# Vision tower on one Trainium2 core: gate products moved into the second half of the image ahead, weighing runs behind the scores

## The chip, the cores and the metric

The kernel runs on one core of one Trainium2 chip. The metric is the device time of one execution, in microseconds (us). Engines are called PE (matmul), PEld (its weight loads), DVE, ACT, POOL and SP (which only issues DMAs).

## What is computed

Eight images of 3 x 512 x 512 go through a patch embedding, one attention layer with a gate, and a layer of eight experts of which one is chosen per token. Everything is fp32 (some matmul operands fp32r). The part that the change touches, cut from the reference:

```python
h = embed(x) + pos                                   # 1024 tokens an image, 256 wide
normed = layernorm(h) ; a = layernorm(normed)        # attention's own layer norm follows the first
q, k, v = split(a * gamma + beta) @ W_qkv.T          # 8 heads of 32
gate = sigmoid(normed @ W_gate.T + b_gate)
attn = softmax(q @ k.T * 32 ** -0.5)
out = einsum('bhij,bhid->bhjd', attn, v) * gate      # weighed over the query tokens i
h = h + normed + out @ W_final.T + b_final
h = h + expert(layernorm(h))                         # router: argmax of softmax(gelu(..) @ Wg)
```

## The kernel before, in words

The eight images are software-pipelined in `image(b, par, before, after)`, which each engine's program has. Image b is in attention; image b + 1 is embedded, normalised, turned and projected meanwhile (`after`); image b - 1 is finished: final product, layer norm, router and hidden layer (`before`). At the end come a sort of the tokens by expert and the expert products, which the change does not touch.

Attention runs in 64 steps (STEPS), one for a head and a tile of 128 tokens: k // 32 is the half (G_STEPS = 32; four heads each), (k % 32) // 4 the tile, k % 4 the head. In a step PE makes the score of 128 x 1024 (L509) in one of two pairs of banks (SR = 2), DVE its maximum (L1066, nmax), ACT the exponential into pr (L854) with its sum. The score of step k waits for the exponential of step k - 2, whose banks it takes. After four steps DVE divides v by the four sums (scale_v, L954 and L957, vs), and PE weighs with it (weigh, L523): 16 products j = 0 to 3 times four heads, in two runs of eight. What else runs in a step is set by tables:

- WEIGH_AT: the runs of group i come at the end of steps 4i + 5 and 4i + 7, behind the step's other work;
- QK1_AT: projections of q and k for the second half in steps 0 to 7; EMBED_AT: embedding of the next image in steps 8 to 31, three pieces a tile (L476, added to hres by DVE, L930);
- GATE_AT: in steps 35 to 38 the gate products of the second feature chunk (L543), each of two steps followed by a tanh on ACT (L803); those of the first chunk stand between the final products (L559) and step 0;
- TURN_AT: in steps 39 to 46 eight turns (L488, four transposes each) of the next image's n and a, read by ACT into nt (L783) and at (L786);
- QK0_AT: in steps 49 to 59 the next image's q and k for its first half (L497): eight products, in two of every three steps, high part by ACT (L797), low part by DVE (L945) two steps later; VALUE_AT: its values (L536) in steps 61 and 63.

Banks 6 and 7 (spare) serve all of that by turns: gates, turns, projections, embedding, values, final products. Each user waits for the reader of the one before.

Ahead of step 0, PE makes values, the last weighings of the image before, and its final products; DVE adds those to hres in four pieces (L973), then does statistics (L908, L915), and only then its first maximum. Ahead of step 32 stand norm_turn (L572, which waits until DVE has added the last embedding, emb_h), the weighing of group 7, and the router of the image before, some 30 us of PE work. SP loads the stacks st, which scores read, by `load_stack`: twelve DMAs, three a head, after the last low part and after the last score of the half before.

## Time and profile before

| | us |
|---|---|
| median of 3 runs | 1819.79 (1818.34 to 1821.87) |
| the profiled execution, its own time | 1824.39 |
| its span, first to last instruction | 1822.6 |
| busy in the span: PE, DVE, ACT, POOL | 1631.2, 1201.0, 943.0, 307.8 |
| mean granted TensorE clock | 0.967 |

A page gives each engine's busy time and the chain of work that ended last. Matmuls are pipelined and their ends modelled, so their rows overlap: the distance of two starts tells more than a row's length. A row of the timeline has start, length, engine, line, operation, output <- input, shapes, count, and in brackets the idle time before it with the engine and line that ended it. A stretch is a window (from:to), its length, the busy time and the number of records of PE, PEld, DVE, ACT and POOL, then the granted clock (PEclk), the DMA share and GB/s. The step of a row is found by counting exponentials.

### The profile page before, as it was taken

What the parts mean: (1) busy time and instruction counts of PE and PEld (TensorE: products, weight loads), DVE (VectorE), ACT (ScalarE), POOL (GpSimd) and SP (SyncE); (2) the same over time, 40 slices, a digit from 0 to 9 for tenths busy, and PEclk for the clock granted to TensorE, in tenths of its full rate; (3) what the DMA queues carried; (4) which work ended last, traced back from release to release, by engine and by line L of the source; (5) the groups of instructions that cost most, each with busy time, mean ns of one, the idle gap of its engine ahead of it and who ended that gap; (6) DMA issues with size and microseconds to landing.
All of it is one profiled execution on the core that took longest, in us unless ns stands there. A gap on an engine that the chain in (4) does not pass through costs nothing.

```text
span 1822.6 us, 29454 instructions
## 1 busy us (share of the span) xinstructions
PE 1631.2 (90%) x11124; PEld 1125.0 (62%) x11124; DVE 1201.0 (66%) x1904; ACT 943.0 (52%) x1560; POOL 307.8 (17%) x231
## 2 busy tenths in 40 slices
PE   8796999999999999999999999998885707999998
PEld 6463556556646665665657456645443506999998
DVE  2376686868777776777677767776666496444443
ACT  0465655756575657567565756575663331222222
POOL 0202000200200020002001000200000081555554
PEclk9798999999999999999999999999999858999999
DMA  4313235242604251342325141603330462666663
GB/s 162 87 53 69 43 94 132 57 99 64 144 19 111 68 147 23 106 117 81 87 67 131 42 110 53 162 5 89 80 83 20 118 163 90 199 202 204 208 198 129
DMA packets 121218, 187.57 MB, mean 103 GB/s; under 512 B 11883, under 2 KB 86265, under 8 KB 120956
## 3 DMA queue, kind: packets, MB, share of 16 engines
q1 hardware_dynamic: 104652, 120.42, 26.7%
q0 software_dynamic: 16000, 63.98, 10.9%
q8 instruction: 93, 1.52, 0.3%
q10 hardware_dynamic: 432, 1.31, 0.2%
q14 instruction: 41, 0.34, 0.1%
HBM read 84.98 MB, written 51.38 MB: 75 GB/s over the span
## 4 chain that ended last, share of the span: by engine, by line
PE 68%; DVE 18%; issue 7%; ACT 5%; DMA 1%; SPq 1%; POOL 0%; POOLq 0%; DVEq 0%; ACTq 0%
PE ps L509 12%; PE ps L752 11%; PE ps L523 11%; PE ps L476 8%; DVE nmax L1066 6%; ACT pr L854 3%; PE ps L740 3%; PE ps L559 3%; PE ps L536 3%; PE ps L497 3%; PE ps L580 2%; PE ps L582 2%; PE ps L581 2%; PE ps L543 1%; PE ps L450 1%
## 5 line engine op out<-in xcount | busy, mean ns | idle before, releaser
L1066 DVE TENSOR_REDUCE nmax<-ps 128x1 f32<-128x1024 f32 x512 | 623.7, 1221 | 216.7 <-PE ps L509 209.8
L854 ACT ACTIVATE pr<-ps,nmax 128x1024 f32<-128x1024 f32 x512 | 570.7, 1115 | 287.1 <-DVE nmax L1066 282.2
L509 PE MATMUL ps<-st 96*128 96x512 f32 x1024 | 399.6, 474 | 70.5 <-ACT pr L854 60.8
L509 PEld LDWEIGHTS ps<-st 96*128 96x128 f32 x1024 | 168.2, 191 | 266.5 <-ACT pr L854 128.6
L523 PE MATMUL ps<-pr,vs 128*32 128x256 f32 x4096 | 271.7, 386 | 11.5 <-DVE vs L957 11.5
L752 PE MATMUL ps<-wd,hg 128*128 x1728 | 224.9, 287 | 0.0
L752 PEld LDWEIGHTS ps<-wd,hg 128*128 128x128 f32 x1728 | 212.2, 192 | 0.0
L523 PEld LDWEIGHTS ps<-pr,vs 128*32 128x32 f32 x4096 | 108.8, 109 | 153.4 <-issue 70.4
L890 ACT ACTIVATE hg<-ps 128x512 fp32r<-128x512 f32 x144 | 78.6, 596 | 239.6 <-PE ps L740 234.8
L476 PE MATMUL ps<-wp,xt 128*128 128x256 f32 x672 | 172.8, 378 | 0.0
L823 ACT ACTIVATE ht<-ps,bf 128x512 f32<-128x512 f32 x128 | 88.3, 690 | 129.8 <-PE ps L582 129.8
L476 PEld LDWEIGHTS ps<-wp,xt 128*128 128x128 f32 x672 | 126.3, 189 | 25.2 <-DVE qk L945 1.2
L497 PE MATMUL ps<-nt,wqk 128*128 128x512 f32 x256 | 132.8, 604 | 3.5 <-DVE qk L945 2.8
L1187 DVE TENSOR_TENSOR hg<-ps,hg 128x512 fp32r<-128x512 f32 x144 | 93.0, 687 | 48.6 <-ACT hg L890 47.3
L354 POOL TENSOR_SCALAR vare<-mv 128x8 f32<-128x8 f32 x8 | 1.9, 240 | 661.4 <-DVE mv L915 661.4
L1194 DVE SCALAR_TENSOR_TENSOR rows<-ps,slot_prob,rows 128x256 f32<-128x256 f32 x72 | 34.9, 484 | 111.4 <-issue 90.0
L580 PE MATMUL ps<-nt_high,wf 128*128 128x512 f32 x256 | 104.4, 408 | 1.7 <-DVE nt_low L994 1.4
L582 PE MATMUL ps<-nt_high,wf 128*128 128x512 f32 x256 | 101.7, 397 | 0.0
L581 PE MATMUL ps<-nt_low,wf 128*128 128x512 f32 x256 | 101.7, 397 | 0.0
L854 ACT ACTIVATION_READ_ACCUMULATOR pr<-ps,nmax 128x1 f32 x512 | 99.6, 195 | 0.0
L417 POOL DMA_INDIRECT out<-rows,slot_to x72 | 72.5, 1007 | 123.8 <-DVE rows L1194 115.6
L346 POOL TENSOR_SCALAR vare<-mv 128x8 f32<-128x8 f32 x8 | 1.9, 238 | 519.7 <-DVE mv L915 519.7
(129 smaller groups left out, 1885.6 us busy)
## 6 DMA issues: line engine op xcount, KB each, us to landing
st<-qk SPq DMA_DIRECT2D x192, 256.0 KB, 5.1
xt<-x_in SPq DMA_DIRECT2D x58, 384.0 KB, 3.1
token_rows<-staged_b SPq DMA_DIRECT2D x64, 256.0 KB, 4.1
token_rows<-staged_a SPq DMA_DIRECT2D x64, 256.0 KB, 4.1
token_rows<-hres POOLq DMA_DIRECT2D x8, 1024.0 KB, 5.2
wd_raw<-w_down SPq DMA_DIRECT2D x64, 128.0 KB, 3.0
pr<-x_in SPq DMA_DIRECT2D x6, 384.0 KB, 9.0
rows<-token_rows,slot_from POOLq DMA_INDIRECT x72
```

The source lines that it names most:

```text
L476: last = mm(spare(t)[:, 0:D], xt[:, t % 2, k, :], wp[:, k, :], start=(k == 0), stop=(k == KC - 1))
L497: last = mm(spare(j), wqk[:, c, w * D + g * P:w * D + (g + 1) * P], nt[:, c, hf * HALF:(hf + 1) * HALF], start=(c == 0), stop=(c == DC - 1))
L509: last = mm(ps[:, 2 * (k % SR) + j, :], stq[:, hh, i * P:(i + 1) * P], stk[:, hh, j * 512:(j + 1) * 512], start=True, stop=True)
L523: last = mm(ps[32 * hh:32 * hh + 32, O_BANK + j // 2, (j % 2) * D:(j % 2 + 1) * D], vs[:, gi % 2, hh, :], pr[:, (4 * gi + hh) % PR, j * D: ...
L580: mm(spare(bank), w_high, nt_high[:, c, half], start=(c == 0), stop=False)
L581: mm(spare(bank), w_high, nt_low[:, c, half], start=False, stop=False)
L582: last = mm(spare(bank), w_low, nt_high[:, c, half], start=False, stop=(c == DC - 1))
L752: mm(o, hg[:, s % 2, h_part, k, :], wd[:, w_part, bass.ds(e, 1), k, :], start=(k == 0 and h_part == w_part), stop=False)
L823: actv(ht[:, k, :], spare(bank), ACT.Gelu, bias=bf1[:, k:k + 1]).then_inc(S["ff_act"], 1)
L854: actv(pr[:, k % PR, :], ps[:, 2 * (k % SR):2 * (k % SR) + 2, :].rearrange("p a n -> p (a n)"), ACT.Exp, bias=nmax[:, k % 16:k % 16 + 1], ...
L1066: V.reduce_max(nmax[:, k % 16:k % 16 + 1], ps[:, 2 * (k % SR):2 * (k % SR) + 2, :].rearrange("p a n -> p (a n)"), AX_X, negate=True).then_ ...
L1187: V.tensor_tensor(hg[:, s % 2, 1, 4 * c:4 * c + 4, :].rearrange("p k n -> p (k n)"), ps[:, 2 * (s % 2) + c, :], high_part.bitcast(F32), AL ...
```

## The change

1. `at` and `gate` become one tensor ga with two slots by image parity. The gate product reads a half of ga, and the tanh writes over that half, once both of its products are done.
2. All gate products of an image (two halves x two chunks x two contraction parts) move into the second half of the image ahead, steps 43 to 46 and 48 to 51, with the tanh in steps 46, 47, 51, 52. Those of image 0 stand ahead of its step 32. None are left ahead of step 0.
3. Turns move to steps 35 to 42; `a` is read by DVE (a copy, turned_a) and no longer by ACT. Projections move to steps 53 to 60, one a step.
4. Weighing runs come behind the score, ahead of the step's other work, one step later: steps 4i + 6 and 4i + 8.
5. load_stack waits for the scores of one head at a time.

```diff
-        at = tensor(sa, "at", [P, DC, TOKENS])
+        ga = tensor(sa, "ga", [P, 2, DC, TOKENS])
...
-        gate = tensor(sa, "gate", [P, DC, TOKENS])
...
-        GATE_AT = {G_STEPS + 3 + m: divmod(m, 2) for m in range(4)}
-        TURN_AT = {G_STEPS + 7 + j: j for j in range(8)}
-        QK0_AT = {G_STEPS + 17 + 3 * j + c: (j, c) for j in range(4) for c in range(2)}
+        TURN_AT = {G_STEPS + 3 + j: j for j in range(8)}
+        GATE_AT = {G_STEPS + 11 + 5 * hf + 2 * c2 + c: (hf, c2, c) for hf in range(2) for c2 in range(2) for c in range(DC)}
+        TANH_AT = {G_STEPS + 14 + 5 * hf + c2: (hf, c2) for hf in range(2) for c2 in range(2)}
+        QK0_AT = {G_STEPS + 21 + 2 * j + c: (j, c) for j in range(4) for c in range(2)}
...
-                        if k == min(4 * i + 5 + j // 2 * 2, (i // TILES + 1) * G_STEPS - 1)] for k in range(STEPS)}
+                        if k == min(4 * i + 6 + j // 2 * 2, (i // TILES + 1) * G_STEPS - 2 + j // 2)] for k in range(STEPS)}
...
-                hold(sp, "score_mm", b * STEPS + g * G_STEPS)
                 for hh in range(4):
+                    wait(sp, "score_mm", b * STEPS + g * G_STEPS - 3 + hh)
...
-                    wait(pe, "tr_read", b * 8 + j - 1)
+                    wait(pe, ("tra_read", "trn_read")[w // 2], b * 4 + (j - 2) // 4 * 2 + j % 2 + 1)
...
+            def gates(b, hf, c2, c):
+
+                if c == 0 and c2 == 0 and hf == 0:
+                    wait(pe, "tra_read", b * 4 + 4)
+                if c == 0 and hf == 1:
+                    wait(pe, "g_tanh", b * 4 + c2 + 1)
+                last = mm(spare(c2), wg[:, c, c2 * P:(c2 + 1) * P],
+                          ga[:, b % 2, c, hf * HALF:(hf + 1) * HALF], start=(c == 0), stop=(c == DC - 1))
                 if c == DC - 1:
                     last.then_inc(S["g_mm"], 1)
...
-                for j in range(2):
-                    if before:
-                        wait(pe, "fin_h", b * 4 - 1 + j)
-                    else:
-                        wait(pe, "v_read", b * 4 + 3 + j)
-                    for c in range(DC):
-                        gates(b, 0, j, c)
                 for k in range(STEPS):
...
+                        if not before:
+                            for hf in range(2):
+                                for c2 in range(2):
+                                    for c in range(DC):
+                                        gates(b, hf, c2, c)
...
                     score(b, k)
+                    for gi, j in WEIGH_AT[k]:
+                        weigh(b, gi, j)
...
+                    if after and k in GATE_AT:
+                        gates(b + 1, *GATE_AT[k])
                     if after and k in QK0_AT:
                         j, c = QK0_AT[k]
-                        if j == 0 and c == 0:
-                            wait(pe, "tr_read", b * 8 + 16)
+                        if j < 2 and c == 0:
+                            wait(pe, "g_tanh", b * 4 + 7 + j)
                         project(b + 1, 0, j, c)
...
-                    for gi, j in WEIGH_AT[k]:
-                        weigh(b, gi, j)
...
+            def gated_tanh(b, hf, c):
+
+
+                wait(act, "g_mm", b * 4 + 2 * hf + 2)
+                actv(ga[:, b % 2, c, hf * HALF:(hf + 1) * HALF], spare(c), ACT.Tanh,
                      bias=hbgate[:, c:c + 1], scale=0.5).then_inc(S["g_tanh"], 1)
...
+            def turned_a(b, j):
+                hf, w = j // 4, j % 4 - 2
+                wait(dve, "tr_mm", b * 8 + j + 1)
+                V.tensor_copy(ga[:, b % 2, w, hf * HALF:(hf + 1) * HALF], spare(j)).then_inc(S["tra_read"], 1)
```

How the rows of PE stand, at three places. First the start of an image, where `wv,nt` is the last values product and `wfin` the final products. Before:

```order
L536 MATMUL ps<-wv,nt 128x128 x8
L559 MATMUL ps<-wfin,gate 128x256 x16
L543 MATMUL ps<-at,wg 128x512 x4
L509 MATMUL ps<-st 128x512 x2
L497 MATMUL ps<-nt,wqk 128x512
```

With the change (its lines are numbered anew):

```order
L536 MATMUL ps<-wv,nt 128x128 x8
L563 MATMUL ps<-wfin,ga 128x256 x16
L509 MATMUL ps<-st 128x512 x2
L497 MATMUL ps<-nt,wqk 128x512
L509 MATMUL ps<-st 128x512 x2
```

The four gate instructions between the final products and the first score are gone; the projections of the first steps follow the first score directly.

Second, PE in the second half from the score of step 35 on, where `wg` is a gate product, `ident` a turn and `pr,vs` a weighing run. Before:

```order
L509 MATMUL ps<-st 128x512 x2
L543 MATMUL ps<-at,wg 128x512
L509 MATMUL ps<-st 128x512 x2
L543 MATMUL ps<-at,wg 128x512
L509 MATMUL ps<-st 128x512 x2
L543 MATMUL ps<-at,wg 128x512
L523 MATMUL ps<-pr,vs 32x256 x8
L509 MATMUL ps<-st 128x512 x2
L543 MATMUL ps<-at,wg 128x512
L509 MATMUL ps<-st 128x512 x2
L488 MATMUL ps<-ident,n 128x128 x4
L523 MATMUL ps<-pr,vs 32x256 x8
```

With the change:

```order
L509 MATMUL ps<-st 128x512 x2
L488 MATMUL ps<-ident,n 128x128 x4
L509 MATMUL ps<-st 128x512 x2
L488 MATMUL ps<-ident,n 128x128 x4
L509 MATMUL ps<-st 128x512 x2
L488 MATMUL ps<-ident,a 128x128 x4
L509 MATMUL ps<-st 128x512 x2
L523 MATMUL ps<-pr,vs 32x256 x8
L488 MATMUL ps<-ident,a 128x128 x4
L509 MATMUL ps<-st 128x512 x2
L488 MATMUL ps<-ident,n 128x128 x4
L509 MATMUL ps<-st 128x512 x2
```

The gate products have left these steps, the turns have come four steps forward, and the weighing of group 8 stands behind the score of step 38 and ahead of its turn.

Third, PE from the score of step 43 on, with the change:

```order
L509 MATMUL ps<-st 128x512 x2
L547 MATMUL ps<-ga,wg 128x512
L509 MATMUL ps<-st 128x512 x2
L523 MATMUL ps<-pr,vs 32x256 x8
L547 MATMUL ps<-ga,wg 128x512
L509 MATMUL ps<-st 128x512 x2
L547 MATMUL ps<-ga,wg 128x512
L509 MATMUL ps<-st 128x512 x2
L523 MATMUL ps<-pr,vs 32x256 x8
L547 MATMUL ps<-ga,wg 128x512
L509 MATMUL ps<-st 128x512 x4
L523 MATMUL ps<-pr,vs 32x256 x8
```

Before, from the score of step 47 on, where the projections (`wqk`) followed the turns:

```order
L509 MATMUL ps<-st 128x512 x2
L523 MATMUL ps<-pr,vs 32x256 x8
L509 MATMUL ps<-st 128x512 x4
L497 MATMUL ps<-nt,wqk 128x512
L523 MATMUL ps<-pr,vs 32x256 x8
L509 MATMUL ps<-st 128x512 x2
L497 MATMUL ps<-nt,wqk 128x512
L509 MATMUL ps<-st 128x512 x2
L523 MATMUL ps<-pr,vs 32x256 x8
L509 MATMUL ps<-st 128x512 x2
L497 MATMUL ps<-nt,wqk 128x512
```

Eight gate products now stand between the last turn and the first projection, one in each of steps 43 to 46 and 48 to 51, with a weighing run ahead of every other one.

## Rows read from the trace of the kernel before

**Rows 1.** The page: busy time, and the chain by engine
```profile
PE 1631.2 (90%) x11124; PEld 1125.0 (62%) x11124; DVE 1201.0 (66%) x1904; ACT 943.0 (52%) x1560; POOL 307.8 (17%) x231
...
PE 68%; DVE 18%; issue 7%; ACT 5%; DMA 1%; SPq 1%; POOL 0%; POOLq 0%; DVEq 0%; ACTq 0%
```

**Rows 2.** Chain of waits at the start of image 3 (start us, us, what)
```profile
563.23 6.92 PE ps L559 x32
...
570.18 0.70 DVE hres L973
...
573.65 0.64 DVE mv L915 x8
574.29 1.12 DVE nmax L1066
```

**Rows 3.** Stretches of image 3: steps 8-30, 35-38, 39-46, 53-60, 35-60
```profile
590.50:634.40 43.90, 43.90 (x325) 29.33 (x327) 33.18 (x46) 27.73 (x46) 0.00 (x0) 1.00 0.18 55
672.60:680.10 7.50, 7.50 (x51) 3.93 (x52) 5.20 (x7) 5.72 (x10) 0.00 (x0) 1.00 0.21 60
680.10:694.50 14.40, 13.21 (x109) 7.29 (x109) 10.35 (x12) 13.64 (x25) 0.00 (x0) 1.00 0.01 1
...
705.70:720.50 14.80, 13.45 (x96) 7.20 (x95) 11.52 (x16) 11.00 (x19) 0.00 (x0) 1.00 0.00 0
672.60:720.50 47.90, 44.28 (x318) 22.76 (x321) 35.60 (x45) 37.99 (x66) 0.00 (x0) 1.00 0.04 10
```

**Rows 4.** Timeline of PE, image 7 (start us, us, ...)
```profile
1287.15 0.73 PE L509 MATMUL ps<-st 96*128 96x512 f32 x2
...
1290.44 0.74 PE L509 MATMUL ps<-st 96*128 96x512 f32 x2 [0.18 <-ACT pr L854]
...
1292.90 1.07 PE L523 MATMUL ps<-pr,vs 128*32 128x256 f32 x16 [0.36 <-DVE vs L957]
1293.90 0.73 PE L509 MATMUL ps<-st 96*128 96x512 f32 x2
```

**Rows 5.** Timeline of PE and DVE at the start of image 3
```profile
569.98 3.60 PE L543 MATMUL ps<-at,wg 128*128 128x512 f32 x8
573.01 1.03 PE L509 MATMUL ps<-st 96*128 96x512 f32 x2
...
574.21 2.42 DVE L1066 TENSOR_REDUCE nmax<-ps 128x1 f32<-128x1024 f32 x2
```

**Rows 6.** Timeline of SP's queue and PE at the start of image 0
```profile
69.26 14.15 SPq L296 DMA_DIRECT2D st<-qk  x12
...
87.28 1.22 PE L509 MATMUL ps<-st 96*128 96x512 f32 x2 [2.48 <-DMA st<-qk]
```

**Rows 7.** Groups by line: ACT's read of a turn (image 3), DVE's copy of a bank (image 2)
```profile
L783 ACT ACTIVATE nt<-ps,vecs 128x512 f32<-128x512 f32 x4 | 3.1, 782 | 0.0
...
L1009 DVE COPY xt<-ps 128x512 f32<-128x512 f32 x1 | 0.7, 673 | 0.0
```

**Rows 8.** Timeline of PE and ACT in the second half of image 3
```profile
681.39 0.73 PE L509 MATMUL ps<-st 96*128 96x512 f32 x2 [0.36 <-ACT pr L854]
...
718.01 0.73 PE L509 MATMUL ps<-st 96*128 96x512 f32 x2 [0.35 <-ACT pr L854]
...
720.50 1.12 ACT L854 ACTIVATE pr<-ps,nmax 128x1024 f32<-128x1024 f32 x1 [0.34 <-DVE nmax L1066]
```

**Rows 9.** Stretch of image 0 before step 32, columns as in rows 3
```profile
147.00:162.00 15.00, 3.19 (x36) 1.53 (x28) 11.30 (x35) 0.78 (x1) 6.44 (x4) 0.75 0.86 183
```

**Rows 10.** Timeline of PE and DVE at the middle of image 2
```profile
464.54 1.07 PE L523 MATMUL ps<-pr,vs 128*32 128x256 f32 x16
465.54 1.97 PE L572 MATMUL ps<-ident,n 128*128 128x128 f32 x16
...
464.92 0.41 DVE L930 TENSOR_TENSOR hres<-ps,posb 128x256 f32<-128x256 f32 x1
```

**Rows 11.** Stretch of image 2, steps 35 to 38, columns as in rows 3
```profile
503.30:512.10 8.80, 8.80 (x52) 4.69 (x52) 5.28 (x6) 5.85 (x10) 0.00 (x0) 0.85 0.11 31
```

69 lines of the change are left out of this document (33 added, 36 removed).

## The prediction

> **What bounds the kernel now.** I read the page first, then the chain of waits around the start of an image, then the timeline of PE, ACT and DVE there, then stretches of one image. PE is busy for 1631.2 of 1822.6 us, and the chain that ended last is 68% PE, 18% DVE and 5% ACT [rows 1]. So for each moved product the question is whether PE sets the end where it leaves and where it arrives. A difference of 0.2%, 3.6 us, is about what a measurement of this kernel can tell from no change.
>
> Image 3 stands for images 1 to 6. Its steps come at three paces. At the start of an image the chain goes through the final products, DVE's last addition to hres, its statistics, and the first maximum [rows 2]; the gate products are not on it. In steps 8 to 30 PE is busy for all of 43.90 us: 23 steps at 1.91, PE is full [rows 3]. In the second half, from the exponential of step 35 to that of step 61, PE is busy for 44.28 of 47.90 us, ACT for 37.99, DVE for 35.60 [rows 3]. There a loop sets the pace: score, maximum, exponential, and the score two steps on in the same bank. Image 7 shows it nearly alone: score 1287.15, score of the same bank 1290.44, 3.29 us for two steps; the next pair takes 3.46, to 1293.90, since a weighing waits 0.36 for vs ahead of a score [rows 4].
>
> **1. The gate products that leave the start of an image: worth nothing.** In image 3 the eight gate records begin at 569.98 and the first score at 573.01 [rows 5], so PE spends 3.0 us there. But DVE makes its last addition at 570.18 and is in its aggregate until 574.29 [rows 2]; the first maximum starts at 574.21, with no idle noted before it [rows 5]. The scores lie ready by then, and the third score waits for the first exponential, now as before. Without the gates the first score is ready 3 us sooner, and DVE still comes at 574.2. Image 0 has another cover: its fourth score waits for its stack until 87.28, 18.0 us after the first load was issued at 69.26 [rows 6], and nothing here issues those loads sooner. Sum: 0. Without that cover it would be 3.0 us for each of seven images (the last rival).
>
> **2. Where they arrive: steps 43 to 52 of the second half, images 0 to 6.** Four products stood in steps 35 to 38, eight stand now in steps 43 to 52. Eight records took about 3.4 us at the start (3.0 to the first score, which overlaps the last of them, whose row ends at 573.58 [rows 5]), so a product of two records is 0.86 and the half gains 4 x 0.86 = 3.4 us of PE work. Floor: PE's idle of 47.90 - 44.28 = 3.6 us takes it all, -0.2. Ceiling: +3.4. By pieces, each from exponential to exponential:
> - Steps 35 to 42 (turns). Before: 7.50 and half of 14.40, 14.7 [rows 3]. Now two of every four reads are DVE's. A step with a read on ACT costs the exponential's 1.1 and the read, whose row has 0.78 but part of which overlaps: about 1.75. A step with a copy on DVE costs the maximum's 1.2, a copy of a bank, 0.67 [rows 7], and some wait for a turn issued behind score and weighing: about 1.95. 4 x 1.75 + 4 x 1.95 = 14.8: +0.1.
> - Steps 43 to 52. In the full stretch a pair of steps, with two embedding pieces (as many columns as two products) and a weighing, takes 2 x 1.91 = 3.82 [rows 3]. Four such pairs are 15.3; steps 47 and 52 have no product: two scores (3.82 - 1.72 - 1.0 leaves 0.55 each) and a weighing, 2.1. That is 17.4. Stepping through with the loop's 3.29 I find 0.3 lost ahead of each of scores 48, 50 and 53, where the gap brings a bank's scores closer than the loop allows, 0.5 at step 43, where the gates wait for DVE's last copy, and 0.4 where a tanh stands ahead of an exponential. 19.2, against half of 14.40 plus the 11.2 that are left of 47.90: 18.4. +0.8.
> - Steps 53 to 60. Eight projections in 8 steps, not in 12: 15.3, and 0.5 for waits on the last tanh and qk's low part. 15.8 against 14.80 [rows 3]: +1.0.
> - Step 61. Its score now comes late from a full PE, and its exponential follows after a bare 2.05 (the loop's 3.29 less the exponential's 1.1 and a handover of 0.1 to 0.2), where it took 2.49 (718.01 to 720.50 [rows 8]): the score is later by another 0.4.
>
> The sum is +2.3 an image, 7 x 2.3 = +16.1. From score 61 to the end of the final products PE has the same work as before and no idle.
>
> **3. Turned read and in-place tanh.** DVE gains 4 x 0.67 an image and has 12 us of room in the stretch [rows 3]; ACT loses as many reads. Their cost is in part 2. Writing the tanh over its source makes it wait for both products of its half; they end before the exponential ahead of it does, so 0. In image 0 the 6.9 us of gates stand ahead of step 32, where PE is busy for 3.19 of 15.00 us and DVE for 11.30 [rows 9]: 0.
>
> **4. Weighing behind the score.** Ahead of score 31 stand 13 weighings, as before, but one moves from the start of the image, which DVE sets, past score 8, where PE is full. Score 8 can come 0.9 sooner and then pays 1.0; with a DVE that holds the next score I take +0.3, bounds 0 and +1.0, images 0 to 6: +2.1. In the middle the last weighing (464.54) stood behind the last embedding product and hid DVE's addition of it (464.92), and the turn began at 465.54 [rows 10]. Now that product ends where the weighing ended, its addition starts near 465.7 and takes 0.41, and the turn begins near 466.2: +0.65, bounds 0 and +1.0, images 1 to 6: +3.9. In the last image 52 steps have no other work, and the 0.17 a group of four lost to vs goes: 13 x 0.15 = -2.0, bounds 0 and -4.
>
> **5. Stack loads by head.** The last low part now falls in step 62, so the loads of the first half start some 2.8 us after score 62. The fourth head needs 18.0 [rows 6], so it is there at 20.8 after score 62 and is wanted at about 24: 0. In the middle only image 0 waited for a load, and there DVE is later [rows 9]: 0. What SP has queued behind them (x tiles, hidden rows) goes out no later than before.
>
> **Sum.** 0 + 16.1 + 2.1 + 3.9 - 2.0 = +20.1 us. The profiled execution took 1824.39 us, so 1844.5 in its terms; the median of the runs is 4.6 lower, 1819.79, and I forecast 1819.8 + 20.1, about **1840 us**.
>
> **Rivals.**
> - *PE's idle takes the products* (0.12). The half costs -0.2: 7 x -0.2 + 2.1 + 3.9 - 2.0 = +2.6, 1822. For it: 3.6 us idle for 3.4 us of work. Against it: the idle lies before scores that wait for an exponential (0.36 at 681.39 [rows 8]), in places of which only some get work. The Trainium skill (Perfetto Trace Analysis, Identifying the Most-Contended Engine) holds that matmul busy time is a poor measure of headroom and wants the share of weight loads, here 22.76 of 47.90 us. By that there is far more room, and this rival's 1822 would be the time to take.
> - *Faster: the weighing leaves the score's loop* (0.11). Before, a weighing of 1.0 us stood ahead of every other score. If the turns then run at the bare loop, 4 x 3.29 = 13.2 for 14.7, the gates at 17.4 for 18.4 and the projections at 15.3 for 14.8, an image gains 2.0, seven 14.0. With the delays of part 4 hidden and the last image's 2.0: 1804. It decides if the exponential of step 43 follows that of step 35 in less than about 14.0. Against it: DVE's copy and ACT's read each lengthen four of the eight steps beyond 1.65.
> - *The clock falls more often* (0.09). In steps 35 to 38 of image 2 the granted clock was 0.85, half speed for a part of them, and they took 8.80 us [rows 11] where image 3 took 7.50 at 1.00 [rows 3]. Products are now gone from these steps and transposes stand there. Five more images at 1.3: +6.5, 1847. Against it: the transposes of the stretch of 14.40 ran at 1.00 [rows 3]. The Trainium skill (TensorE: Matmul & The Clock Gate, Part 4: PE-mode transpose) says that a transpose does not count as activity for the clock. By that rule this rival would be the likely case.
> - *The start was on the path after all* (0.04): 7 x 3.0 less, 1819. The chain speaks against it [rows 2].
>
> **How the numbers follow.** The forecast has 0.64; its own range, with part 2 between 1.4 and 3.4 an image, is 1832 to 1850. The range of all, 1814 to 1852, takes in the first and the last rival and stops above the faster one; its high end is the ceiling of part 2, or the clock. Faster: 0.11 and a little of the last rival, 0.12. Same: most of the first and the last, 0.14. Slower: the rest, 0.74.
>
> **What would show it.** Start of an image: PE idle about 3 us more before the third score, and no less time from the last final product to the first maximum. Steps 35 to 61: about 49.8 us, PE idle under 3. Middle: the turn waits for hres, 0.65. I am wrong if steps 35 to 61 take under 48 us, or if the start shrinks.

## The result, and the profile after

The changed kernel is slower: 1861.16 us, median of 4 runs, where the kernel before took 1820.83 beside it (4 runs). The ratio is 1.0209, 95% interval 1.0188 to 1.0231. The forecast was 1840 with a range up to 1852: the direction is right, the forecast size is half of what came.

The page of the changed kernel, on the lines that answer to [rows 1], with the chain by engine and the group of the scores:

```profile
span 1861.3 us, 29441 instructions
...
PE 1666.1 (90%) x11124; PEld 1141.5 (61%) x11124; DVE 1231.9 (66%) x1936; ACT 928.4 (50%) x1528; POOL 307.1 (17%) x231
...
PE 74%; DVE 15%; issue 5%; ACT 4%; DMA 1%; SPq 1%; POOL 0%; POOLq 0%; DVEq 0%
...
L509 PE MATMUL ps<-st 96*128 96x512 f32 x1024 | 448.9, 523 | 79.2 <-ACT pr L858 73.2
```

The same group in the page of before:

```profile
L509 PE MATMUL ps<-st 96*128 96x512 f32 x1024 | 399.6, 474 | 70.5 <-ACT pr L854 60.8
```

The number of PE's instructions is the same, 11124, and PE is busy for 34.9 us more than the 1631.2 of [rows 1]. The products did not multiply; their records got longer: a score's lasted 474 ns on average and lasts 523 now. The reader's first question is therefore the granted clock. It was 0.967 over the execution before and is 0.947 now. The six images 1 to 6, from the first exponential of image 1 to that of image 7, as one stretch of the kernel before (start:end and length, then busy time of PE, PEld, DVE, ACT and POOL with counts, granted clock, DMA share, GB/s):

```profile
238.00:1248.80 1010.80, 968.87 (x6433) 606.81 (x6432) 743.11 (x1201) 629.00 (x1045) 92.70 (x49) 1.00 0.35 87
```

and of the changed kernel:

```profile
241.20:1282.90 1041.70, 990.33 (x6432) 616.45 (x6432) 766.40 (x1225) 619.13 (x1020) 92.64 (x49) 0.97 0.34 85
```

These six images hold 30.9 of the 38.7 us by which the span grew. The rest: image 0, +5.6, less 2.4 that its first exponential comes sooner; image 7 from its first exponential to its last, +0.9; and the part behind it, in which the change touches nothing, 436.4 where it was 432.8. (That last part came out anywhere between 428.7 and 438.0 in the profiled executions of this study, also 432.4 in a descendant of the changed kernel, a_gap. It tends to be longer where TensorE ran longer at half clock, 85 us here against 76, and was not tested by itself.)

Image 3 of the changed kernel, stretch by stretch, in the columns of [rows 3]: 5.4 us before its first exponential, steps 0 to 7, steps 8 to 30, the middle pause, steps 35 to 42, steps 43 to 52, steps 53 to 60, and all from 35 to 60:

```profile
581.20:586.60 5.40, 2.79 (x9) 1.29 (x7) 5.16 (x19) 0.00 (x0) 0.95 (x2) 1.00 0.69 198
586.60:603.30 16.70, 15.01 (x63) 7.62 (x64) 13.51 (x20) 11.52 (x20) 1.89 (x2) 0.80 0.19 64
603.30:647.90 44.60, 44.60 (x329) 29.56 (x328) 34.00 (x46) 27.77 (x47) 0.00 (x0) 1.00 0.31 82
647.90:682.10 34.20, 32.87 (x192) 23.40 (x190) 25.41 (x61) 16.83 (x24) 10.39 (x5) 1.00 0.56 133
686.90:703.10 16.20, 15.30 (x95) 8.83 (x96) 12.87 (x16) 11.99 (x21) 0.00 (x0) 0.81 0.07 19
703.10:722.00 18.90, 18.56 (x118) 8.10 (x117) 13.41 (x16) 13.96 (x24) 0.00 (x0) 1.00 0.00 1
722.00:737.80 15.80, 15.80 (x106) 8.01 (x105) 12.43 (x15) 11.63 (x21) 0.00 (x0) 1.00 0.00 1
...
686.90:737.80 50.90, 49.66 (x316) 24.93 (x317) 38.71 (x47) 37.59 (x64) 0.00 (x0) 0.94 0.02 7
```

Two of these stretches have a granted clock of 0.80 and 0.81. In the kernel before the same two stood at 1.00:

```profile
575.40:590.50 15.10, 13.78 (x67) 6.61 (x66) 13.56 (x20) 11.60 (x20) 1.91 (x2) 1.00 0.21 71
...
672.60:687.30 14.70, 14.27 (x107) 7.77 (x108) 10.37 (x13) 12.54 (x22) 0.00 (x0) 1.00 0.11 31
```

The clock has two levels, 1.2 and 2.4 GHz. Cut closer, the changed kernel ran at the lower one right behind the first exponential of the image, and again from step 34 on, behind the router:

```profile
587.20:594.00 6.80, 6.03 (x10) 3.24 (x11) 4.20 (x6) 4.43 (x8) 1.29 (x2) 0.50 0.44 154
679.30:686.20 6.90, 5.67 (x38) 2.96 (x36) 6.47 (x9) 5.01 (x7) 4.89 (x2) 0.99 0.88 233
686.20:693.00 6.80, 6.36 (x31) 3.88 (x30) 5.25 (x7) 5.35 (x10) 0.00 (x0) 0.51 0.25 72
```

I call such a piece of half clock a spell. Each of images 1 to 6 of the changed kernel has one at its start and one behind its router, 12 spells with 61 us; the same images of the kernel before have two spells with 7 us, both behind a router (images 2 and 5, [rows 11]).

What PE did ahead of the spell at the start is the part that the change made. The chain of waits at the start of image 3 now (start us, us, what):

```profile
574.42 6.92 PE ps L563 x32
...
581.37 0.70 DVE hres L982
...
582.09 2.72 DVE bst L912 x8
...
584.83 0.64 DVE mv L919 x8
585.48 1.12 DVE nmax L1077
...
586.62 1.21 ACT pr L858 x2
...
587.97 1.19 PE ps L509 x2
589.16 1.71 PE ps L497 x2
```

and PE's timeline of the same place:

```profile
580.98 0.82 PE L509 MATMUL ps<-st 96*128 96x512 f32 x2
581.64 1.02 PE L497 MATMUL ps<-nt,wqk 128*128 128x512 f32 x2
582.10 1.03 PE L509 MATMUL ps<-st 96*128 96x512 f32 x2
582.97 1.02 PE L497 MATMUL ps<-nt,wqk 128*128 128x512 f32 x2
587.97 1.19 PE L509 MATMUL ps<-st 96*128 96x512 f32 x2 [3.98 <-ACT pr L858]
588.96 1.91 PE L497 MATMUL ps<-nt,wqk 128*128 128x512 f32 x2
```

From DVE's last addition to the first exponential it is 5.25 us (581.37 to 586.62), and 5.25 before (570.18 in [rows 2], exponential at 575.43). The removal at the start bought nothing there, as forecast: the two scores lie ready and DVE's statistics set the pace. But PE, which had stood idle 0.56 us before its third score, now stands idle 3.98, and the pair of projections that took 1.02 takes 1.91 behind it. The third score of before:

```profile
576.78 0.70 PE L509 MATMUL ps<-st 96*128 96x512 f32 x2 [0.56 <-ACT pr L854]
```

In the middle, the turn waits for DVE's last embedding sum:

```profile
647.49 1.13 PE L476 MATMUL ps<-wp,xt 128*128 128x256 f32 x4
649.13 1.97 PE L576 MATMUL ps<-ident,n 128*128 128x128 f32 x16 [0.52 <-DVE hres L934]
```

### The profile page after: what moved, and what is told of

It reads as the page before. It is cut to its first block, busy times and chain, and to the rows that moved or that the text cites. A ratio compares the mean times of both kernels' runs of the same rounds, so it can differ in the third digit from the quotient of the medians.

```text
span 1861.3 us, 29441 instructions
## 1 busy us (share of the span) xinstructions
PE 1666.1 (90%) x11124; PEld 1141.5 (61%) x11124; DVE 1231.9 (66%) x1936; ACT 928.4 (50%) x1528; POOL 307.1 (17%) x231
## 4 chain that ended last, share of the span: by engine, by line
PE 74%; DVE 15%; issue 5%; ACT 4%; DMA 1%; SPq 1%; POOL 0%; POOLq 0%; DVEq 0%
PE ps L509 12%; PE ps L523 11%; PE ps L758 11%; PE ps L476 9%; PE ps L497 6%; DVE nmax L1077 5%; ACT pr L858 4%; PE ps L746 3%; PE ps L563 3%; PE ps L536 3%; PE ps L584 3%; PE ps L586 3%; PE ps L585 3%; PE ps L547 2%; PE ps L450 1%
## 5 line engine op out<-in xcount | busy, mean ns | idle before, releaser
L509 PE MATMUL ps<-st 96*128 96x512 f32 x1024 | 448.9, 523 | 79.2 <-ACT pr L858 73.2
L509 PEld LDWEIGHTS ps<-st 96*128 96x128 f32 x1024 | 189.0, 202 | 246.1 <-ACT pr L858 114.2
L523 PE MATMUL ps<-pr,vs 128*32 128x256 f32 x4096 | 275.7, 390 | 2.1 <-DVE vs L966 2.1
L476 PE MATMUL ps<-wp,xt 128*128 128x256 f32 x672 | 182.0, 393 | 0.0
L476 PEld LDWEIGHTS ps<-wp,xt 128*128 128x128 f32 x672 | 119.8, 189 | 53.4 <-issue 34.6
L497 PE MATMUL ps<-nt,wqk 128*128 128x512 f32 x256 | 150.0, 675 | 2.1 <-DVE qk L954 0.9
```

The lines of the kernel that those rows point to most:

```text
L476: last = mm(spare(t)[:, 0:D], xt[:, t % 2, k, :], wp[:, k, :], start=(k == 0), stop=(k == KC - 1))
L497: last = mm(spare(j), wqk[:, c, w * D + g * P:w * D + (g + 1) * P], nt[:, c, hf * HALF:(hf + 1) * HALF], start=(c == 0), stop=(c == DC - 1))
L509: last = mm(ps[:, 2 * (k % SR) + j, :], stq[:, hh, i * P:(i + 1) * P], stk[:, hh, j * 512:(j + 1) * 512], start=True, stop=True)
L523: last = mm(ps[32 * hh:32 * hh + 32, O_BANK + j // 2, (j % 2) * D:(j % 2 + 1) * D], vs[:, gi % 2, hh, :], pr[:, (4 * gi + hh) % PR, j * D: ...
```

## The experiments

The table gives each kernel with its ratio to the kernel before on the same chip and what one image takes there. Beside the experiments the kernel before took 1823.3 to 1824.5 us, so a median is not to be divided by the 1820.83 of the first row. Times of an image are between its exponentials, read from ACT's timeline, of image 3 unless noted. "start" is exponential 0 to 8, "first half" 0 to 31, "middle" 31 to 32, "second half" 32 to 63, "end" 63 to the next 0. The last two columns are the spells in images 1 to 6 and the length of those six images.

| kernel | median us | ratio [95%] | start | first half | middle | second half | end | spells 1-6 | images 1-6 us |
|---|---|---|---|---|---|---|---|---|---|
| before | 1820.83 | 1 | 15.1 | 59.0 | 33.5 | 56.7 | 18.9 | 2 | 1010.8 |
| changed | 1861.16 | 1.0209 [1.0188, 1.0231] | 16.7 | 61.2 | 34.3 | 59.8 | 19.5 | 12 | 1041.7 |
| a_fill | 1848.30 | 1.0141 [1.0122, 1.0161] | 14.7 | 59.3 | 34.3 | 58.6 | 19.4 | 4 | 1030.3 |
| a_fill2 | 1848.25 | 1.0118 [1.0090, 1.0145] | 14.7 | 59.3 | 34.3 | 58.7 | 19.4 | 2 | 1030.9 |
| b_thin_start | 1837.05 | 1.0066 [1.0048, 1.0085] | 16.4 | 60.3 | 33.5 | 57.9 | 18.9 | 12 | 1023.6 |
| b_thin_mid | 1845.55 | 1.0128 [1.0109, 1.0146] | 15.1 | 59.0 | 33.5 | 59.2 | 18.9 | 6 (10.2 us each) | 1023.3 |
| b_weigh | 1826.02 | 1.0009 [0.9998, 1.0019] | 14.7 | 59.2 | 34.3 | 55.3 | 19.5 | 3 | 1013.6 |
| a_oldweigh | 1891.60 | 1.0366 [1.0343, 1.0389] | 17.2 | 61.0 | 33.5 | 62.6 | 20.0 | 12 | 1067.0 |
| b_mix | 1814.97 | 0.9939 [0.9919, 0.9959] | 15.1 | 59.0 | 33.5 | 55.3 | 19.5 | 0 | 1003.9 |
| b_turn | 1831.44 | 1.0022 [1.0006, 1.0039] | 15.1 | 59.0 | 33.5 | 57.0 | 18.9 | 5 | 1016.3 |
| b_defer | 1839.55 | 1.0070 [1.0054, 1.0086] | 15.9 | 60.3 | 33.5 | 58.0 | 18.8 | 6 | 1023.6 |
| a_defer | 1833.58 | 1.0044 [1.0028, 1.0060] | 15.6 | 60.1 | 34.3 | 59.5 | 16.1 | 6 | 1017.1 |
| b_gap | 1824.44 | 0.9997 [0.9982, 1.0011] | 14.6 | 59.0 | 33.5 | 56.7 | 18.8 | 2 | 1010.5 |
| a_gap | 1834.55 | 1.0052 [1.0033, 1.0072] | 15.6 | 60.1 | 34.3 | 58.8 | 17.5 | 7 | 1022.0 |
| a_best | 1835.52 | 1.0059 [1.0037, 1.0080] | 16.0 | 60.5 | 33.5 | 60.8 | 17.5 | 10 | 1024.9 |
| b_best | 1810.36 | 0.9915 [0.9890, 0.9941] | 14.6 | 59.0 | 33.5 | 55.4 | 19.4 | 0 | 1003.7 |
| b_best_fill | 1812.30 | 0.9932 [0.9911, 0.9954] | 14.6 | 59.0 | 33.5 | 55.8 | 19.4 | 0 | 1006.5 |

Kernels with a_ start from the changed kernel, those with b_ from the kernel before. The theory after the result: what the change costs beyond its work is TensorE's clock, which falls once PE has nothing to do at the start of the image, and again behind the router. The rival: the second half is overfull by more than was worked out, and the clock is a bystander.

**Put other work where the gates stood (a_fill).** Four products that nobody reads, of the shape of those that left, in their old place:

```diff
                 if before:
                     final(b - 1)
+                for j in range(2):
...
+                    for c in range(DC):
+                        mm(spare(j), wg[:, c, 0:P], ga[:, b % 2, c, j * HALF:(j + 1) * HALF],
+                           start=(c == 0), stop=(c == DC - 1))
                 for k in range(STEPS):
```

> The changed kernel with four products of two parts each put back ahead of step 0 as pure filler (their result is overwritten unread). Clock theory: the trace of the changed kernel has a stretch of half clock of 3.4 to 6.8 us at the start of each of images 1 to 7, because PE idles 4 us there while DVE runs its statistics; with the filler PE is busy, these stretches go, and the time falls by about 1.6 us an image, 10 to 12 us in all, although 3.4 us of PE work an image are added: 1850. Rival (the moved work itself costs, the clock only follows): no change or up to 3 us slower, 1861 to 1864.

It got faster by adding work: 1.0141 where the changed kernel stands at 1.0209, with intervals that do not meet. The start of image 3 (the same two stretches as above, then steps 35 to 60):

```profile
576.50:581.90 5.40, 5.40 (x16) 2.75 (x15) 5.21 (x19) 0.05 (x1) 1.02 (x2) 1.00 0.68 202
581.90:596.60 14.70, 13.39 (x65) 6.24 (x64) 13.45 (x20) 11.58 (x21) 1.82 (x2) 1.00 0.21 72
...
680.10:729.90 49.80, 48.69 (x317) 24.45 (x318) 38.69 (x47) 37.72 (x65) 0.00 (x0) 0.97 0.03 7
```

PE is busy through the first, the third score waits 0.54 for ACT's exponential instead of 3.98, steps 0 to 7 take 14.7 for 16.7, and no image start has a spell. Two images (2 and 5) have no spell at all: 171.2 us each, second half 58.2. They show the changed order without the clock (the filler in it is covered, as the gates were): 3.2 us over the 168.0 of an undisturbed image before.

**Take the start gates' work away, and nothing else (b_thin_start).** In the kernel before, the products of the start are cut to 8 of their 512 columns (this leaves out most of the gate values of the first channel chunk); those of steps 35 to 38 stay whole:

```diff
-                last = mm(spare(hf), wg[:, c, c2 * P:(c2 + 1) * P],
-                          at[:, c, hf * HALF:(hf + 1) * HALF], start=(c == 0), stop=(c == DC - 1))
+                width = 8 if c2 == 0 else HALF
+                last = mm(spare(hf)[:, 0:width], wg[:, c, c2 * P:(c2 + 1) * P],
+                          at[:, c, hf * HALF:hf * HALF + width], start=(c == 0), stop=(c == DC - 1))
```

> The kernel before with the gate products ahead of step 0 narrowed to 8 of 512 columns (the gate of the first feature chunk is then wrong data; nothing is added elsewhere). Clock theory: half clock at the start of images 1 to 7, 1.6 us each, so 10 to 12 us slower than before although work was taken out: 1831. Rival, my prediction's step 1 as it stood (removal at the start is worth exactly nothing): 1820 within 2 us. Second rival (the products were on the path): 3.0 us each, 1799.

Less work, and 1.0066 slower. PE's timeline at the start of image 3 of this run:

```profile
573.90 1.03 PE L509 MATMUL ps<-st 96*128 96x512 f32 x2
574.76 1.02 PE L497 MATMUL ps<-nt,wqk 128*128 128x512 f32 x2
578.29 0.96 PE L509 MATMUL ps<-st 96*128 96x512 f32 x2 [2.50 <-ACT pr L855]
579.05 1.91 PE L497 MATMUL ps<-nt,wqk 128*128 128x512 f32 x2
```

The idle time is 2.50 and a spell of 3.4 us follows in every image: start 16.4 for 15.1. A spell of 3.4 us also stands behind every router now, though nothing was changed there: steps 35 to 42 went from 14.7 to 15.9. That is the cleanest proof that the removal by itself is not worth 0 but costs: 12.8 us over six images, 8.1 of it at the starts and the rest behind the routers, two of which had a spell before. No part of this kernel is fuller than before, so here the clock is no bystander and the rival falls.

**The gates that left steps 35 to 38 (b_thin_mid).** The same edit with `c2 == 1`: the start is whole, the products of steps 35 to 38 have 8 columns (most of the second chunk's gate values are left out).

> The kernel before with the gate products of steps 35 to 38 narrowed to 8 of 512 columns. Clock theory: the stretch behind the router is now thinner, so the half clock that only images 2 and 5 had there comes in most images, 1.3 to 1.5 us each in five more: plus 5 to 7 us, less up to 0.7 us an image of the shorter steps; 1821 to 1825. Rival (clock does not depend on these products): time falls by 0.5 to 0.7 us an image, 1815 to 1817, with low clock in two images as before.

1.0128, far above the 1821 to 1825 us expected: the direction of the clock theory is right, but it had reckoned with the short spell of before. Steps 35 to 42 of image 3 take 17.2 us for 14.7, at a granted clock of 0.70, and each of images 1 to 6 has a spell of 10.2 us there:

```profile
676.60:693.80 17.20, 16.07 (x106) 9.70 (x106) 10.46 (x12) 12.76 (x22) 0.00 (x0) 0.70 0.08 21
```

So both places from which the change took products kept the clock up. The changed kernel has shorter spells behind the router than this run (3.4 and 6.8 us); its turned reads and weighing stand elsewhere too, and which of these shortens them was not tried apart.

**Fill both places (a_fill2).** a_fill with one more filler behind the partial logits of step 33:

```diff
                         partial_logits(b - 1, 1, 0)
+                        for c in range(DC):
+                            mm(spare(1), wg[:, c, 0:P], wqk[:, c, 0:HALF], start=(c == 0), stop=(c == DC - 1))
```

> The changed kernel with two groups of products that nobody reads: the four ahead of step 0 of an earlier run, and two more behind the partial logits of step 33. Theory A (of the changed kernel's 41 us over the one before, the half clock takes the half, at the start of each image and behind the router, and the rest is added work in the second half and in the two pauses): with both places filled the spells behind the router go too, every image takes about 171.2 us as the undisturbed ones of the run with the first filler did, against 168.0 before, 7 x 3.2 = 22 us, so 1845 us on a chip where the kernel before takes 1823; 1.3 us more in each image where a spell stays. Theory B (the spells behind the router come from the gates' absence at steps 35 to 38, whatever stands at step 33): as with the first filler alone, 1848 us, 9 spells. Theory C (all of the excess is the clock's): 1823 to 1828.

The routers of images 1, 3, 4 and 6, which had a spell in a_fill, have none; images 2 and 5, which had none, have one. An undisturbed image is 171.7, 0.5 longer for the filler, which is all that the clock gives back, so the six images come out the same, 1030.9 for 1030.3. This run, with hardly a spell in the images, is 1.0118 of the kernel before; the forecast was 1840 / 1819.8 = 1.0111. The two ratios of the filled kernels, 1.0118 and 1.0141, can't be told apart, since their intervals overlap.

**The weighing (b_weigh, a_oldweigh, b_mix).** b_weigh moves the weighing of the kernel before behind the score, with the change's table, and nothing else:

```diff
-                        if k == min(4 * i + 5 + j // 2 * 2, (i // TILES + 1) * G_STEPS - 1)] for k in range(STEPS)}
+                        if k == min(4 * i + 6 + j // 2 * 2, (i // TILES + 1) * G_STEPS - 2 + j // 2)] for k in range(STEPS)}
...
                     score(b, k)
+                    for gi, j in WEIGH_AT[k]:
+                        weigh(b, gi, j)
...
-                    for gi, j in WEIGH_AT[k]:
-                        weigh(b, gi, j)
```

a_oldweigh is the reverse, the changed kernel with the weighing in its old places. b_mix is b_weigh for the second half alone: groups under TILES keep the old step and place, the others get the new:

```diff
                     score(b, k)
+                    for gi, j in WEIGH_AT[k]:
+                        if gi >= TILES:
+                            weigh(b, gi, j)
...
                     for gi, j in WEIGH_AT[k]:
-                        weigh(b, gi, j)
+                        if gi < TILES:
+                            weigh(b, gi, j)
```

> The kernel before with the weighing runs alone moved behind the score, one step later. My step 4: plus 0.65 us at the middle of images 1 to 6 (the turn waits for hres), plus 0.3 in the first half, minus 2 in the last image; the second half, which has a loop with slack, gains 0 to 1 us an image. Sum plus 4 to minus 4: 1816 to 1824. Rival (the order of weighings carries a large part of the 40 us): over 1828.

> The changed kernel with the weighing runs back at the ends of steps 4i + 5 and 4i + 7. Weighing theory (my step 4): the 0.65 to 0.8 us at the middle of images 1 to 6 goes and the last image is 2 us longer: 3 us faster than the changed kernel, 1858, and the half-clock stretches stay. Rival (the second half needs the new order, since a full PE no longer hides a weighing ahead of a score): 3 to 8 us slower than the changed kernel.

> The kernel before with the weighing behind the score in the second half alone. Theory A (this is what makes the faster version fast): second half 56.7 to 55.3, last pause 18.9 to 19.5, so 0.8 an image and 1.3 in images 2 and 5 where no spell comes: 1812 to 1820, a ratio of 0.994 to 0.998. Theory B (it needs the statistics moved as well, for the clock): spells stay behind the routers, ratio 0.998 to 1.001.

b_weigh is 1.0009, a little above the expected 1816 to 1824 us: two effects that cancel. Middle +0.8 (33.5 to 34.3), first half +0.3, second half -1.4 and the end +0.6, so 168.4 for 168.0. The gain is where nothing but the loop sets the pace; steps 43 to 52 and 53 to 60 of b_weigh's image 3:

```profile
686.00:703.70 17.70, 16.47 (x124) 7.89 (x128) 14.04 (x18) 14.42 (x25) 0.00 (x0) 1.00 0.00 1
703.70:717.90 14.20, 13.37 (x100) 6.90 (x93) 11.60 (x16) 10.85 (x20) 0.00 (x0) 1.00 0.00 0
```

against 18.4 and 14.80. In the fuller second half of the changed kernel it is worth much more: a_oldweigh is 1.0366, some 29 us slower than the changed kernel, where 3 us faster was expected and 3 to 8 slower by the rival. With the weighing put back, steps 53 to 60 take 17.80 for 15.80, and PE, though it has the same work as in the changed kernel, is idle 2.6 us there:

```profile
737.00:754.80 17.80, 15.18 (x88) 7.24 (x88) 12.07 (x15) 11.50 (x22) 0.00 (x0) 1.00 0.00 0
```

Image 3 of a_oldweigh has no spell behind its router, and its second half is 62.6 us: 4.4 more than the 58.2 of an undisturbed changed image, with less half clock in images 1 to 6 than the changed kernel (54 against 61 us). This loss is therefore the order's and not the clock's.

b_mix takes the gain and leaves the loss at the middle: 167.3 in every image from 1 to 6, no spell in them, 0.9939. About 4 of its 6.9 us over these images are the order, the rest are the two spells of before that don't come. So of the change's parts this one, in one half only, was worth having.

**The turned reads (b_turn).** The four reads of a turned `a` move from ACT to DVE in the kernel before, with a semaphore of their own for each engine:

```diff
+            def turned_a(b, j):
+                hf, w = j // 4, j % 4 - 2
+                wait(dve, "tr_mm", b * 8 + j + 1)
+                V.tensor_copy(at[:, w, hf * HALF:(hf + 1) * HALF], spare(j)).then_inc(S["tra_read"], 1)
...
+                    if after and k in TURN_AT and TURN_AT[k] % 4 >= 2:
+                        turned_a(b + 1, TURN_AT[k])
```

> The kernel before with only the read of the turned a moved from ACT to DVE. Theory: ACT limits steps 39 to 46 (13.64 of 14.40 us busy); with four reads fewer each image gains up to 0.6 us, 0 to 4 us in all: 1819 against 1823 on this chip. Rival: DVE's copy waits for the turn and delays the next maximum by as much; no change, or up to 3 us slower.

An undisturbed image is 168.3, +0.3; images 1 and 2 have two spells each in the second half (170.9). Together that is 5.5 us over six images, and no gain of the kind expected. The ratio of 1.0022 also has in it a longer part behind the last image (438.0 us for 432.8 in the profiled execution), which the edit doesn't touch.

**DVE's statistics out of the start (b_defer, a_defer, b_gap, a_gap, a_best).** If DVE's statistics are the cover, the removal must pay once they are gone. In the two `defer` kernels they go into steps 0 to 3, two tiles a step, with the aggregate in step 4 and the normalised tiles at steps 7, 10, 13 and on (POOL's store of the finished rows also goes ahead of its root of the variance, so that it doesn't wait for it):

```diff
-        NORM_AT = {2 + t: t for t in range(TILES)}
+        STAT_AT = {k: (2 * k, 2 * k + 1) for k in range(TILES // 2)}
+        NORM_AT = {7 + 3 * t: t for t in range(TILES)}
...
-                    stats_3(b - 1, 1 - par)
...
+                    if before and k in STAT_AT:
...
+                        for t in STAT_AT[k]:
+                            last = V.bn_stats(bst[:, 2, t, :], hres[:, 1 - par, t, :])
...
+                    if before and k == TILES // 2:
+                        aggregate(b - 1, 3)
```

In the `gap` kernels they stand between the four residual additions, and only the last two tiles and the aggregate behind them; the normalised tiles come at the same later steps:

```diff
                     V.tensor_tensor(h[:, j * 512:(j + 1) * 512], h[:, j * 512:(j + 1) * 512], spare(j), ALU.add
                                     ).then_inc(S["fin_h"], 1)
+                    wait(dve, "fin_h", b * 4 + j + 1)
+                    for t in range(2 * j, 2 * j + 2):
+                        last = V.bn_stats(bst[:, 2, t, :], hres[:, par, t, :])
+                last.then_inc(S["stats3"], 1)
```

a_best is a_gap with the weighing of the first half back in its old place.

> The kernel before with the statistics of the finished image taken out of the stretch ahead of step 0 (two tiles a step in steps 0 to 3, aggregate in step 4) and its normalisation spread over steps 7 to 28. Theory: DVE sets the start of an image; the first maximum then follows the last addition or the first score (PE, after its gates), 0.4 us sooner, and steps 0 to 8 lose 1.0 to 1.4 us of DVE work: 8 to 12 us faster than before. Rival: the products around step 0 set the pace too, under 3 us faster.

> The changed kernel with the same deferral. Theory: DVE was the cover of the removed gate products, and PE's 4 us idle there dropped the clock. Without the statistics ahead of step 0 the first exponential comes some 3.3 us sooner, PE does not idle, the half clock at the image starts goes (1.6 us), steps 0 to 8 gain 1: 5 to 6 us an image for images 1 to 7, 35 to 42 us: 1819 to 1826, which makes the removal worth its 3 us. Rival (only the clock mattered, not DVE's cover): as much as the filler gave, 11 to 13 us: 1848.

> The kernel before, with the statistics of each two tiles taken between the four residual additions of the final product (only the last pair and the aggregate stand behind the last addition) and the norm's tiles at steps 7, 10, 13 ... Theory A (VectorE's statistics are what the first exponential of an image waits for only as long as the start gates do not last as long; with the gates at the start TensorE idles 0.56 us there, so not more than that is to be won there): exponential 63 to the next 0 from 18.9 to about 18.0 and the first eight steps 15.1 to 14 or 15, so 0 to 1.8 us an image, 1811 to 1823 on a chip where before takes 1823, less 1.6 us for each image start at which the granted clock falls. Theory B (any work of VectorE moved out of the start starves TensorE at the start, as the run with deferred statistics did, 1.007): 1830 to 1838, a spell behind every router.

> The changed kernel with the statistics of each two tiles between the four residual additions, norms at steps 7, 10, 13 ... Theory A (VectorE's statistics behind the final product are the cover that made the start gates' removal worthless): the pause from exponential 63 to the next 0 falls from 19.5 to 16 or 17, no half clock at the image start, so images of 168 to 170 us: 1828 to 1840 on a chip where before takes 1823; 1.3 us more for each spell that stays behind a router. Theory B (the four additions themselves are the chain, each behind its product on TensorE): the pause falls by 1 us or less, the spells at the start stay, 1850 to 1860.

> The run before this one with the weighing of the first half back at its old places. Theory A: the middle pause returns to 33.5 (from 34.3), 0.8 an image less: 1822 to 1834, about the kernel before and slower than the kernel before with the same two edits (0.9915), since the fuller second half still costs its 1.6 us and the spells stay behind the routers. Theory B (moving the gates was good but for the statistics): under 1810.

With the gates at the start there is nothing to win from DVE: b_gap is 0.9997, the end is 18.8 as before and the start is 0.5 shorter, of which nothing is left at step 31. b_defer only lengthens the start (15.9) and has a spell behind every router: 8 to 12 us faster was expected and under 3 faster by the rival, and it came out 0.7% slower, so both failed. b_gap came out just above its range, and its rival of a spell behind every router did not come. Without the gates there is: the end of the image falls from 19.5 to 16.1 in a_defer and to 17.5 in a_gap, and 1.0209 becomes 1.0044 and 1.0052 (for a_defer between its expectation, 1819 to 1826 us, and its rival, 1848). The end and the first eight steps of a_gap, image 1, which has no spell (169.0 us in all):

```profile
234.10:239.50 5.40, 4.77 (x18) 3.03 (x16) 4.79 (x17) 0.00 (x0) 0.93 (x2) 1.00 0.95 238
239.50:254.00 14.50, 12.58 (x63) 6.30 (x64) 11.94 (x16) 11.52 (x20) 2.09 (x2) 1.00 0.25 87
```

PE's third score of image 3, in a_gap and in a_defer:

```profile
580.20 0.82 PE L509 MATMUL ps<-st 96*128 96x512 f32 x2 [2.04 <-ACT pr L858]
574.96 0.71 PE L510 MATMUL ps<-st 96*128 96x512 f32 x2 [0.59 <-ACT pr L859]
```

So the cover was DVE's statistics, and taking it away turns the removal into 3.4 us at the end of an image (a_defer, which gives 0.8 back by step 31, 60.1 for a_fill's 59.3) or 2.0 (a_gap). In a_gap about 2.0 us of idle time are left before the third score, and a spell follows in four of six images; the expectation had none there. Over all runs the start of images 1 to 6 sorts by this idle time: at 0.5 to 0.6 us no image has a spell there, at 2.0 four of six have one (a_gap, a_best), at 2.5 and at 4.0 every one (b_thin_start, the changed kernel, a_oldweigh). Even so no a_ kernel comes under the one before: an undisturbed image of a_gap is 169.0 for 168.0, and spells remain in most. a_best shows how the clock takes what an edit gives. Its middle is back at 33.5, 0.8 an image less, as expected, but it has spells of 10.2 us behind two routers and of 6.8 behind three, and its six images are 2.9 us longer than a_gap's. Its expectation of 1822 to 1834 was missed by a little.

**The version that beats both (b_best, b_best_fill).** b_gap and b_mix together, and the same with a filler at step 33.

> The kernel before with the statistics between the additions as in the run of that alone, and with the weighing behind the score in the second half only (the first half keeps its places). Theory A (weighing behind the score is worth 1.4 us in the second half, 56.7 to 55.3, and costs 0.8 in the middle pause only through the first half's last groups): per image -1.4 beside what the statistics bring, 165.5 to 167.5 against 168.0, so 1806 to 1820 on a chip where before takes 1823, if the granted clock falls no oftener than before. Theory B (the gain is given back in the pause of the image's end, 18.9 to 19.5, and by spells of 1.3 us behind the routers): no change, 1820 to 1828, with more than 10 spells.

> The kernel of the run before this one with two products that nobody reads behind the partial logits of step 33. Theory A (the spells behind the router start in the thin work round the router, and two products of 0.22 us each at full clock keep it busy enough): no spell behind a router in images 1 to 6, each image 0.4 us longer for the products and 1.3 us shorter where a spell stood: 1800 to 1815. Theory B (the fall is decided elsewhere, the products only cost): the same spells as without them and 0.4 x 7 = 3 us slower.

b_best is 0.9915, the fastest of all by its median. Image 3, steps 0 to 7, 35 to 42, 43 to 52 and 53 to 60:

```profile
569.70:584.20 14.50, 13.67 (x67) 6.67 (x67) 12.22 (x15) 11.55 (x20) 0.00 (x0) 1.00 0.21 73
...
666.90:681.70 14.80, 13.88 (x96) 7.20 (x99) 10.46 (x12) 12.67 (x22) 0.00 (x0) 1.00 0.10 28
681.70:699.50 17.80, 16.57 (x128) 7.95 (x131) 14.09 (x19) 14.46 (x26) 0.00 (x0) 1.00 0.01 1
699.50:713.60 14.10, 13.24 (x99) 6.80 (x92) 11.48 (x15) 10.80 (x19) 0.00 (x0) 1.00 0.00 0
```

Its images are those of b_mix (1003.7 and 1003.9 for six), so the statistics add nothing measurable there; the two intervals overlap, and the profiled executions differ in image 7 and behind it. The filler had no spell left to remove and cost 0.47 an image.

## Why the prediction was wrong

**Step 1, the removal at the start, worth 0: this is the step that failed.** Its reading of the path was right. DVE's statistics cover the gates: 5.25 us from addition to exponential before and after, and a_defer and a_gap show that the cover is mostly these. In image 0, too, the cover held: the first exponential comes 2.4 us sooner (77.8 for 80.2; a_fill, with products there again, has 80.2), but the one of step 2 stands at 87.3 with a_fill's at 87.4. What it left out is that the gates, while nobody waited for them, kept PE busy. It named the cover of the removed work, and not what the removed work covered. PE's idle before the third score rose from 0.56 to 3.98 us (the prediction said about 3 more: right), and at that point TensorE goes to half clock. The price is 1.3 us in the start alone for 3.4 us of half clock (b_thin_start) and 2.0 for 6.8 us (image 3, 16.7 against a_fill's 14.7). Over images 1 to 6 the starts of the changed kernel take 9.6 us more than six of a_fill's. b_thin_start adds that the same removal also brings a spell behind each router, 1.2 us there. So the term of 0 should have been a cost of 9.6 us in six images at the least, about half of what the forecast lacks.

**The rival of the clock had the right kind, the wrong place and too small a chance.** It looked for more falls in steps 35 to 38 alone, gave 1.3 in five more images, 6.5 in all, and had 0.09. Behind the router the spells came as it said, in all six images, but they cost less (0.3 to 0.5 us with a short spell, 1.6 with one of 6.8: steps 35 to 42 at 15.0 or 15.1 and at 16.2 against 14.6), 4.9 us in all, where the two of before had cost 2.8. At the start nobody looked. Together: 1041.7 - 6 x 171.2 = 14.5 us in images 1 to 6, of which 2.8 were there before. That is 11.7 of the 30.9, and the forecast's 19.5 for the other terms (below) leaves nothing over.

What argued against this rival in the prediction, transposes that ran at 1.00 in steps 39 to 46 [rows 3], is true and beside the point. In a_fill2 four images ran all of steps 35 to 42, with a transpose in each, at 1.00, and b_thin_mid fell to 0.70 with transposes in steps 39 to 42 only. The Trainium skill (TensorE: Matmul & The Clock Gate, Part 4: PE-mode transpose) says that a transpose does not count as busy for the clock in the way of a product; these runs neither need the rule nor contradict it, since scores stand between all of them.

**Step 2, the second half, +2.3 an image: too high by 0.8.** The undisturbed images (a_fill's 2 and 5) have a second half of 58.2, +1.5. By pieces: turns -0.1 (forecast +0.1), steps 43 to 52 19.0, +0.6 (forecast +0.8), steps 53 to 60 15.8, +1.0 (forecast +1.0). The 0.4 of step 61 did not come: from exponential 61 to 63 it is 4.1 us before and now. The end of the image is 0.6 longer, where the prediction had "no idle" and the same work; but b_weigh and b_mix, which moved no product, have the same 0.6, so that is the weighing's. Steps 35 to 60 together were forecast at 49.8; undisturbed they take 49.4. What the prediction had not seen is that this sum hides two large terms: b_weigh shows -1.4 for the weighing, so the moved products and turns cost 2.9 beside it (58.2 for 55.3), most of their 3.4. With the old order of weighing they cost far more, 6.0 in the second half and 1.1 at the end (a_oldweigh's image 3, 62.6 and 20.0 for 56.7 and 18.9): the two moves hang together, and the prediction priced them apart.

**Step 3, turned reads and in-place tanh, 0 beside step 2**: b_turn gives +0.3 with the old order of weighing. **Step 4, the weighing**: first half +0.3 (forecast +0.3), middle +0.8 (forecast +0.65, the turn waits 0.52 for hres), and the 0.6 at the end, for which the prediction has no term. In the last image b_weigh's first half is 54.1 for 55.3, and its second 52.6 for 52.4, at -1.0 for a forecast of -2.0; but the kernel before has a spell in the first half there and b_weigh one in each. **Step 5, stack loads by head, 0**: it had no run of its own; images 1 to 6 without a spell are accounted for without it.

The sum of the terms without the clock, 19.5 us for images 1 to 6, is measured at 6 x 3.2 = 19.2. For these images the forecast is the changed kernel without its spells. That the sum meets so closely is in part luck: an image of step 2 was 0.8 too high, and one of step 4 0.7 too low (1.7 for 0.95), most of it the end that it left out. Of the 18.6 us by which the span grew beyond the forecast's 20.1, 11.4 lie in images 1 to 6, 0.6 in image 0, 2.9 in image 7 (2.0 of them at its start, 16.7 for a_fill's 14.7), and 3.7 behind the images, where the change touches nothing and the cause stays open.

The other rivals: *PE's idle takes the products* was wrong as to the time: undisturbed, PE's idle in steps 35 to 60 fell from 3.6 to 1.8 us, but the half grew by 1.5 all the same, and by 2.9 of the 3.4 added against the same order of weighing. The Trainium skill (Perfetto Trace Analysis, Identifying the Most-Contended Engine) would have us read headroom off the weight loads, 22.76 of 47.90 us [rows 3]; here, where each score waits for an exponential two steps back, that room was not to be had. *The start was on the path* was wrong; only with the statistics out of the way is there something to win at the start. *The weighing leaves the loop* was half right: the effect is there, 1.4 us in b_weigh, but its condition, exponential 35 to 43 in under 14.0, was not met (14.6).

## What to carry to other kernels

Work that nobody waits for can still be what holds the clock up: before taking it away, ask what the engine does in its place, and charge the next few microseconds at half speed if the answer is "wait". When a kernel has a place where TensorE idles for a few microseconds (2 to 4 here) ahead of dense work, look at the granted clock on both sides of it; a product that nobody reads is the quick test. A change made of several moves should be tried move by move, and also with and without the others: here the weighing, in one half of its range, was worth 0.6% by itself, and without it the moved products cost 7.1 us an image where they cost 2.9 with it.

## What was not expected of the hardware

Adding four useless products an image, of about 0.86 us each, made a kernel faster, from 1.0209 to 1.0141 of the same reference.

A spell far from an edit comes and goes with it. b_thin_start changed nothing between step 31 and 43 and got a spell of 3.4 us behind every router; b_defer likewise, without one at its starts; b_mix, with other places for the weighing, has none in images 1 to 6. What decides whether one comes behind the router was not settled: with the filler at step 33 (a_fill2) the four images that had one in a_fill lost it, and the two that had none got one, though all six run the same program. PE's longest idle piece ahead of that spell in image 3 of b_thin_start is 1.2 us, 2.0 us ahead of the exponential of step 34, and the kernel before, which has no spell in that image, has the same piece there.

Half clock cost less than its length suggests. The 61 us of it in images 1 to 6 of the changed kernel, which at half speed is up to 30 us of TensorE's work undone, cost 14.5. A part of the rest fell on time in which PE waited anyway: its idle in steps 35 to 60 is 1.8 us without a spell (a_fill's images 2 and 5) and 1.2 with one of 6.8 us. Where the remainder went was not tested.
